# Groups of eight, four and two blocks in the gather of a relational graph layer, and other places for its short passes and weight pieces

## What is computed

```python
def _rgcn(x, edge_index, edge_type, weight, root, bias):
    src, dst = (edge_index[0], edge_index[1])
    msgs = x[src]
    out = x @ root + bias
    n = x.shape[0]
    for r in range(weight.shape[0]):
        mask = (edge_type == r).astype(x.dtype)
        sums = jax.ops.segment_sum(msgs * mask[:, None], dst, num_segments=n)
        cnt = jax.ops.segment_sum(mask, dst, num_segments=n)
        mean = sums / jnp.maximum(cnt, 1.0)[:, None]
        out = out + mean @ weight[r]
    return out
u = _rgcn(x, edge_index, edge_type, weight, root, bias)
z = jnp.concatenate([u, x], axis=1) @ w_gate + b_gate
h = jnp.tanh(u) * z + x * (1.0 - z)
```

## Time and profile before

| | us |
|---|---|
| median of 3 runs | 2188.13 |
| lowest and highest | 2180.44, 2189.11 |
| the profiled execution | 2187.53 |
| its span, first to last instruction | 2185.7 |
| mean granted TensorE clock | 0.956 of full |
| busy PE, DVE, ACT, POOL | 2011.1, 1284.4, 969.2, 904.0 |

### The profile page before, as it was taken

How to read it: one execution, slowest core, us unless ns; L and a number is a source line. 1 busy time by engine, 2 the same in 40 slices (tenths; PEclk the granted TensorE clock), 3 DMA queues, 4 the chain that set the end, 5 groups by cost and what they waited for, 6 DMA issues and landing times. The chain is left out here.

```text
span 2185.7 us, 28064 instructions
## 1 busy us (share of the span) xinstructions
PE 2011.1 (92%) x9425; PEld 1596.2 (73%) x9425; DVE 1284.4 (59%) x2282; ACT 969.2 (44%) x1506; POOL 904.0 (41%) x801
## 2 busy tenths in 40 slices
PE   8999999999999999999899899899799579899970
PEld 6777778778888888877677577677488468788860
DVE  8589588832222222139899899899798742222215
ACT  3211122222222222249899799899644223233332
POOL 0000046565655555237677588688200022212212
PEclk9999999999999999999899899999799779999995
DMA  5224487777777877679889799899565579998439
GB/s 185 100 81 134 137 272 247 259 251 253 254 258 259 256 258 256 227 223 321 273 292 315 242 329 319 272 331 313 194 178 176 199 266 326 305 318 287 103 75 188
DMA packets 156848, 520.96 MB, mean 238 GB/s; under 512 B 30748, under 2 KB 31132, under 8 KB 154672
## 3 DMA queue, kind: packets, MB, share of 16 engines
q1 hardware_dynamic: 85616, 310.51, 41.1%
q0 software_dynamic: 71104, 208.84, 32.1%
HBM read 383.83 MB, written 154.68 MB: 246 GB/s over the span
## 5 line engine op out<-in xcount | busy, mean ns | idle before, releaser
L211 PE MATMUL psum<-w_hi,xnT_hi 128*128 128x512 f32 (+1 forms) x1592 | 421.1, 399 | 4.6 <-PEq L228 2.5
L211 PE MATMUL psum<-w_lo,xnT_hi 128*128 128x512 f32 (+1 forms) x1592 | 417.8, 393 | 0.0
L211 PE MATMUL psum<-w_hi,xnT_lo 128*128 128x512 f32 (+1 forms) x1592 | 413.7, 394 | 0.0
L882 POOL DMA_INDIRECT sorted_rows<-acc x313 | 342.9, 1096 | 116.7 <-issue 85.3
L580 ACT ACTIVATE work<-psum 128x512 f32<-128x512 f32 (+1 forms) x150 | 89.7, 598 | 661.5 <-PE psum L211 661.5
L211 PEld LDWEIGHTS psum<-w_hi,xnT_hi 128*128 128x128 f32 (+1 forms) x1592 | 293.5, 187 | 75.4 <-issue 4.0
L211 PEld LDWEIGHTS psum<-w_lo,xnT_hi 128*128 128x128 f32 (+1 forms) x1592 | 294.9, 185 | 73.2
L211 PEld LDWEIGHTS psum<-w_hi,xnT_lo 128*128 128x128 f32 (+1 forms) x1592 | 294.3, 185 | 71.1
L982 POOL DMA_INDIRECT w_hi<-y_rows,sort_row x168 | 221.2, 1317 | 78.3 <-PE psum L1115 41.3
L982 POOL DMA_INDIRECT w_lo<-y_rows,sort_row x164 | 217.9, 1329 | 77.2 <-PE psum L1115 38.6
L1108 PE MATMUL psum<-y_hi,hot 128*128 128x512 f32 x664 | 220.0, 414 | 30.2 <-ACT y_hi L1030 27.4
(11 more groups left out here) (334 smaller groups left out, 2614.0 us busy)
## 6 DMA issues: line engine op xcount, KB each, us to landing
split_experts<-acc SPq DMA_DIRECT2D x128, 512.0 KB, 4.2
ring<-split_experts SPq DMA_DIRECT2D x16, 4096.0 KB, 16.1
w_raw<-in_wchunks SPq DMA_DIRECT2D x86, 512.0 KB, 5.0
y_rows<-work SPq DMA_DIRECT2D x144, 256.0 KB, 2.8
acc<-in_wchunks SPq DMA_DIRECT2D x64, 512.0 KB, 6.0
work<-local_rows SPq DMA_DIRECT2D x26, 384.0 KB, 4.2
sum_rows<-work SPq DMA_DIRECT2D x22, 256.0 KB, 4.5
acc<-in_bias SPq DMA_DIRECT2D x10, 512.0 KB, 5.5
```

What stands on the lines that cost most here:

```text
L211: i = pe.matmul(to[:rm, :], x_[:, k, m * P:m * P + rm], w_[:, s, k * HALF:(k + 1) * HALF], start=(n == 0), stop=(n == 3 * KD - 1))
L882: pool.indirect_dma_start(sorted_dram, IndirectOffsetOnAxis(ap=e_dest[:, c:c + 1], axis=0), e_rec[:, c, :], None, bounds_check=BLOCKS * P ...
```

## The change

The 332 blocks are grouped otherwise: 34 groups of eight blocks, 10 of four and 10 of two (at most one of four and one of two per tile), 54 groups in all. There are still 44 passes, of two "quads" each: a quad is four blocks (or two in a short pass), and a group of eight is the two quads of one pass, which sum in the same pair of banks (`BEGINS`, `ENDS`, `PAIR`) and are flushed once. Passes with two groups of four are 4, 10, 21, 32 and 39; short passes with two groups of two are 5, 11, 22, 33 and 43. In a short pass six matmuls of the unit stand between a block's high and low matmuls, so a unit still fits. The piece passes 8, 19, 30, 41 now have eight blocks: pieces 0 and 1 are split ahead of block 1, piece 2 ahead of block 6 and piece 3 ahead of block 7.

The sort has to find two kinds of rest per tile. `starts()` is cut into `starts()` at (1, 5), `shifts()` at (1, 8) and `owners()` at (3, 8), each with more small operations; `positions` has two more operations over 313 columns per tile, and takes one tile per step from (2, 1) to (3, 0).

```diff
-SHORT = GROUP // 2
-SHORT_GROUPS = TILES
-LONG_GROUPS = -(-((EDGES + TILES * (SHORT * P - 1)) // (SHORT * P) - SHORT_GROUPS) // 4) * 2
-GROUPS = LONG_GROUPS + SHORT_GROUPS
-BLOCKS = LONG_GROUPS * GROUP + SHORT_GROUPS * SHORT
+LONG, SHORT = 2 * GROUP, GROUP // 2
+SIDE_GROUPS = 2 * TILES
+LONG_GROUPS = -(-((EDGES + TILES * (SHORT * P - 1)) // (SHORT * P) - 3 * TILES) // 4)
+GROUPS = LONG_GROUPS + SIDE_GROUPS
+BLOCKS = LONG_GROUPS * LONG + TILES * GROUP + TILES * SHORT
+QUADS = 2 * LONG_GROUPS + SIDE_GROUPS
...
-                    link(v.tensor_scalar(t_odd_i, t_int, 1, None, ALU.bitwise_and))
+                    link(v.tensor_scalar(t_bit, t_int, 1, None, ALU.bitwise_and))
+                    link(v.tensor_copy(t_odd, t_bit))
+                    link(v.tensor_scalar(t_int, t_int, 1, None, ALU.logical_shift_right))
+                    link(v.tensor_scalar(t_bit, t_int, 1, None, ALU.bitwise_and))
+                    link(v.tensor_copy(t_mid, t_bit))
...
+                def shifts():
+                    v.tensor_tensor(mid_used, t_mid_start[:, TILES - 1:TILES], t_mid[:, TILES - 1:TILES], ALU.add)
+                    link(v.tensor_tensor(long_used, t_start[:, TILES - 1:TILES], t_groups[:, TILES - 1:TILES], ALU.add))
+                    v.scalar_tensor_tensor(out=t_mid_at, in0=t_groups, scalar=float(LONG * P), in1=t_off,
...
+                def owners():
+                    side = slice(LONG_GROUPS, GROUPS)
+                    v.tensor_scalar(side_odd, group_f[:, side], -1.0, float(GROUPS - 1), ALU.mult, ALU.add)
+                    v.tensor_scalar(side_mid[:, 0:TILES], group_f[:, LONG_GROUPS:LONG_GROUPS + TILES], float(-LONG_GROUPS), None, ALU.add)
...
                 def positions(first, last):
                     for t in range(first, last):
                         link(v.tensor_scalar(e_mask, e_tile, float(t), None, ALU.is_equal))
                         link(v.tensor_tensor_scan(e_scan, e_ones, e_mask, 0.0, ALU.mult, ALU.add))
-                        link(v.tensor_scalar(e_tail, e_scan, t_tail[:, t:t + 1], t_shift[:, t:t + 1], ALU.is_gt, ALU.mult))
+                        v.tensor_scalar(e_tail, e_scan, t_mid_at[:, t:t + 1], t_mid_shift[:, t:t + 1], ALU.is_gt, ALU.mult)
+                        link(v.tensor_scalar(e_last, e_scan, t_odd_at[:, t:t + 1], t_odd_shift[:, t:t + 1], ALU.is_gt, ALU.mult))
                         link(v.tensor_tensor(e_scan, e_scan, e_tail, ALU.add))
+                        link(v.tensor_tensor(e_scan, e_scan, e_last, ALU.add))
                         link(v.scalar_tensor_tensor(out=e_scan, in0=e_scan, scalar=t_off[:, t:t + 1], in1=e_mask,
                                                     op0=ALU.add, op1=ALU.mult))
...
-                side = {(HIST_CHUNK, 3): [turned], (HIST_CHUNK, 5): [starts],
-                        (HIST_CHUNK + 1, 2): [lambda: positions(0, 3)], (HIST_CHUNK + 1, 6): [lambda: positions(3, 6)],
-                        (HIST_CHUNK + 2, 0): [lambda: positions(6, 8)], (HIST_CHUNK + 2, 2): [lambda: positions(8, TILES)],
-                        (HIST_CHUNK + 2, 4): [records], (LOOK_CHUNK, 0): [table]}
+                side = {(HIST_CHUNK, 3): [turned], (HIST_CHUNK, 5): [starts], (HIST_CHUNK, 8): [shifts],
+                        (HIST_CHUNK + 2, 4): [records], (HIST_CHUNK + 2, 8): [owners], (LOOK_CHUNK, 0): [table]}
+                for t in range(TILES):
+                    side[(HIST_CHUNK + 1 + (t + 1) // TILES, (t + 1) % TILES)] = [lambda t=t: positions(t, t + 1)]
...
-        SHORT_PASSES = (*PIECES_AT, PASSES - 1)
-        ORDER, FIRST, COLUMN = [], [0], []
+        SHORT_PASSES = (*(i + 3 for i in PIECES_AT if i + 3 < PASSES), TILES // 2, PASSES - 1)
+        MID_PASSES = (*(i - 1 for i in SHORT_PASSES[:-1]), PASSES - 5)
+        assert not {*SHORT_PASSES, *MID_PASSES} & {*PIECES_AT}
+        KIND = [SHORT if i in SHORT_PASSES else GROUP if i in MID_PASSES else LONG for i in range(PASSES)]
+        BASE = {LONG: 0, GROUP: LONG_GROUPS * LONG, SHORT: LONG_GROUPS * LONG + TILES * GROUP}
+        NUMBER = {LONG: 0, GROUP: LONG_GROUPS, SHORT: LONG_GROUPS + TILES}
+        taken = {kind: 0 for kind in BASE}
+        OWNER, BEGINS, ENDS, PAIR, FIRST, COLUMN, pair = [], [], [], [], [0], [], -1
         for i in range(PASSES):
             for h in range(2):
-                short = i in SHORT_PASSES
-                n = sum((g >= LONG_GROUPS) == short for g in ORDER)
-                at, size = (LONG_GROUPS * GROUP + n * SHORT, SHORT) if short else (n * GROUP, GROUP)
-                ORDER.append(LONG_GROUPS + n if short else n)
-                COLUMN += range(at, at + size)
+                kind = KIND[i]
+                begins, ends = kind < LONG or h == 0, kind < LONG or h == 1
+                n, part = taken[kind], h * GROUP if kind == LONG else 0
+                pair += begins
+                OWNER.append(NUMBER[kind] + n)
+                BEGINS.append(begins)
+                ENDS.append(ends)
+                PAIR.append(pair)
+                at = BASE[kind] + n * kind + part
+                COLUMN += range(at, at + min(kind, GROUP))
                 FIRST.append(len(COLUMN))
+                taken[kind] += ends
         assert sorted(COLUMN) == list(range(BLOCKS))
 
         def size_of(g):
 
             return FIRST[g + 1] - FIRST[g]
 
-        def pieces_in(i):
-
-            return [(PIECES_AT[i], q) for q in range(PIECES)] if i in PIECES_AT else []
+        PIECES_BEFORE = {1: (0, 1), 6: (2,), 7: (3,)}
+
+        def pieces_in(i, n=None):
+
+            if i not in PIECES_AT:
+                return []
+            return [(PIECES_AT[i], q) for q in (range(PIECES) if n is None else PIECES_BEFORE.get(n, ()))]
...
-                        if pieces:
-                            c, q = pieces[n]
+                        for c, q in pieces_in(i, n):
                             act.wait_ge(mm_done, c * TILES)
                             hi_piece(act, c, 0, q)
...
-                        if g >= 1:
+                        if g >= 1 and ENDS[g - 1]:
                             flush(g - 1)
...
-                        if g >= 2:
-                            pe.wait_ge(acc_done, ACC_NO[g - 2])
+                        if BEGINS[g] and PAIR[g] >= 2:
+                            pe.wait_ge(acc_done, ACC_NO[PAIR[g] - 2])
+                        two = 2 * (PAIR[g] % 2)
...
-                            for _ in itertools.islice(steps, 3 * KD // SLOTS):
+                            for _ in itertools.islice(steps, 3 * KD // (FIRST[2 * i + 2] - FIRST[2 * i])):
```

More of the change, by code:

```diff
@@ L1065, in _ @@
                             b = j % SLOTS
-                            if pieces:
-                                lo_piece(v, pieces[j - FIRST[2 * i]][0], 0, pieces[j - FIRST[2 * i]][1])
+                            for c, q in pieces_in(i, j - FIRST[2 * i]):
+                                lo_piece(v, c, 0, q)
                             v.wait_ge(hi_done, j + 1)
@@ L1104, in _ @@
                             b, k = j % SLOTS, j - FIRST[g]
-                            first, last = k == 0, k == size_of(g) - 1
+                            first, last = BEGINS[g] and k == 0, ENDS[g] and k == size_of(g) - 1
                             pe.wait_ge(hi_done, j + 1)
                             for q in range(2):
-                                o = pe.matmul(bank[2 * h + q], hot[:, h, k, :], y_hi[:, j % 2, q * HALF:(q + 1) * HALF],
+                                o = pe.matmul(bank[two + q], hot[:, h, k, :], y_hi[:, j % 2, q * HALF:(q + 1) * HALF],
                                               start=first, stop=False)
                             o.then_inc(hi_used, 1)
-                            for _ in itertools.islice(steps, 3 * KD // SLOTS):
+                            for _ in itertools.islice(steps, 3 * KD // (FIRST[2 * i + 2] - FIRST[2 * i])):
                                 pass
@@ L1114, in _ @@
                             for q in range(2):
-                                o = pe.matmul(bank[2 * h + q], hot[:, h, k, :], slot_of(b)[:, q * HALF:(q + 1) * HALF],
+                                o = pe.matmul(bank[two + q], hot[:, h, k, :], slot_of(b)[:, q * HALF:(q + 1) * HALF],
                                               start=False, stop=last)
```

89 lines of the change are left out of this document (54 added, 35 removed).

## The result

| | before | after |
|---|---|---|
| median of the runs, us | 2189.1 (2180.4 to 2194.4, 9 runs) | 2175.4 (2172.6 to 2181.6, 9 runs) |
| ratio, 95% interval | 1 | 0.9948 [0.9933, 0.9964] |
| profiled execution, us | 2187.5 | 2177.2 |
| its span, us | 2185.7 | 2175.4 |
| first `y_hi` of the gather stage | 966.0 | 976.7 |

The change is worth 0.5% (11.4 us by the ratio); the time is 3.4 us above the forecast of 2172. But the two stages didn't both do what was forecast. The gather stage became 21.25 us shorter, and it begins 10.65 us later.

The account below looks back on a forecast made before the run. VectorE was taken to bound root passes and TensorE zx passes, with ACT close. Terms -3.3 - 15.6 - 6.2 + 1 + 1 + 6.7 = -16.4 gave 2171.1, 2172 as median; own range 2165 to 2179, wider range 2161 to 2184.

Parts of the forecast that it names:

- (a): Gather stage: 34 of 88 flushes go; 11 root passes gain 0.3 us each, 3.3 us in all, zx passes nothing.
- (b): Gather stage: product passes 5, 11, 22, 33 become short, 9.4 us each; 15.6 us gained.
- Rival 5: Root passes: the flush was not what set them, so the flush gain is 0; 2175 us, chance 0.07.
- Rival 4: Short passes aren't short, 10.9 us each from bank and one-hot turnaround; 6 us more, 2178, chance 0.08.
- The floor of 13.04 for a pass of 56 matmuls: Gather stage, TensorE: 8 x 1.63 us, below which a pass of 56 matmuls can't go.
- (c): Piece passes 8, 19, 30, 41 with eight blocks: the four places take 170.7 us against 176.9; 6.2 gained.
- (d): Half clock of TensorE at the piece passes: 0 to 2.5 us at each place, 1 us lost in all taken.
- (e): Transfers in piece passes: twelve of 512 KB at 374 GB/s may come late; 1 us lost in all, bounds 0 to 10.
- Rival 2: Piece passes bound in part by transfers at 325 GB/s; 9 us more, 2181, chance 0.12.
- rival 3: Piece passes: third piece's load queues behind gathers, landing over 6 us later than the 9.0 of before; 2201 us, chance 0.06.
- (f): Sort's side work on DVE: TensorE stands 5.2 us ahead of chunk 3, then 1.5 of half clock; 6.7 us lost.
- Rival 1: Front: TensorE doesn't stop ahead of chunk 3, so that loss falls to 0; 2165 us, chance 0.17.

Follow-up runs that it names:

- placement_only: Kernel before, with its groups of four and its front, but the new placement of short and piece passes; ratio to before 0.9943.
- grouping_only: Changed kernel with its groups of eight and its front, but the old placement of short and piece passes; ratio to before 1.0028.
- warm_pad: warm with group_tile made 34 unused words longer, so xnT stands where it does in the kernel before; 2160.5 us, ratio to before 0.9886.
- warm: spaced with 16 extra matmuls, results unused, in each piece pass (8, 19, 30, 41); 2163.4 us, ratio to before 0.9906.
- late_pieces: spaced with the third and fourth weight piece both ahead of block 7 of the piece passes; 2171.1 us, ratio to before 0.9942.
- spaced: Changed kernel with the sort's positions moved later, mostly one in every other step, records and owners at (3, 9); 2168.8 us, ratio to before 0.9911.

## Why the prediction held, point by point

The time was in the range and the sign right, but more than a third of the forecast gain didn't come: against the profiled execution, -16.4 was forecast and -10.3 measured. Terms that were 8.2 us too good were met by gains that were 2.1 better than forecast, and 3.2 of the 8.2 stand in no term of the sum. The gains and the stop were foreseen with their mechanism; that the time fell within the range owes something to its width of 14 us.

**Flushes (a) and short passes (b).** Right, and slightly under-sized. Passes 0 to 3 and 13 to 17 gained 3.9 us (0.4 each, not 0.3), the zx passes nothing. The four short places gained 17.1 us, of which (a) had put 0.6 on passes 6 and 12, so 16.2 was forecast. Together 21.0 against 18.9 (15.6 and 3.3). Rival 5, that the flush didn't set the root passes, is out: with 88 flushes (placement_only) they take 13.4, with 54 (grouping_only) 12.99. Rival 4, short passes of 10.9 us, is out too: it would have cost 6 us there. The floor of 13.04 for a pass of 56 matmuls was slightly high: such passes take 12.99, and 12.92 in warm_pad.

**Piece passes (c) and half clock (d).** Here the sum was wrong by 4.0 us: -6.2 with +1 and +1 was forecast, the changed kernel shows -0.2. The engines' work was sized rightly: (c) said 170.7 us for the four places, and at full clock they take 172.0 and 171.5. The step that failed is (d): "I take 1 in all" from a bound of 0 to 2.5 at each place, with the reason that twice the matmuls would shorten the half clock. They did shorten it: over the piece pass and the one behind, the granted clock is 0.84 to 0.89 in the changed kernel (0.83 to 0.95 in its second trace) and 0.66 to 0.81 in the kernel before. It still cost 4.9 us. The kernel before spent more time at the low clock, 0.50 for 17 us, while ACT and DVE waited for a load there; that these waits hid it, and that the full pass has none left to hide it in, is argued and wasn't tried. By the Trainium skill, "TensorE: Matmul & The Clock Gate", "Part 1", an array that idles falls to 1.2 GHz and runs its next matmuls at that; the windows at 0.66 and 0.50 agree.

**Transfers (e).** Between 1088 and 1095 us the queues moved 413 GB/s, and warm held 374 over 29.37 us of a piece pass and the one behind. So the 325 of the zx passes is no ceiling. Nor is the 358 that the prediction weighed, from the Trainium skill, "DMA: Bandwidth & Descriptors", "Where 436 GB/s comes from". The Trainium skill, "HBM Reference", "Specifications (TRN2)", has a core that streams alone well above its share, at about 425; these rows agree. Rival 2 is out, and so is rival 3: the third piece was taken 10.5 us behind the first (9.0 before), 1.5 later and not 6, and late_pieces shows that even its wait cost nothing.

**Front (f).** The mechanism and its place were right: a single stop, ended by the split of chunk 3's fourth piece, 5.0 us where 5.2 was counted; a position took 4.17 us (180.74 to 184.91 in order of time), 4.2 was counted. Half clock behind it cost 2.2 and not 1.5 (the unit takes 8.34 us, 208.93 to 217.27, where it took 6.11), since the second group of eight products was slow too; the three other traces with the stop show 1.4 to 2.7 for it. The second unit comes 7.4 us later than without the stop, against 6.7. Rival 1, that the front doesn't stop, is out.

**Not in the sum.** 3.2 us for the place of the buffers behind `group_tile` in SBUF. The prediction held matmuls for unchanged because their count and shapes were.

The sum of the misses: -2.1 (a, b), +4.0 (c to e), +0.7 (f), +3.2 (address), +0.3 behind the stage: 6.1, the difference of -16.4 and -10.3. It is the account of one pair of executions. Between the two traces of one kernel the first `y_hi`, the piece places and the part behind the stage differ by 0.2 to 2.4 us each, so a single term of it is known to 1 or 2 us.

**Chances.** The rival of chance 0.17, that the front doesn't stop, would have made 2165; spaced shows what that is worth, 2168.8.

## What to carry to other kernels

Where three engines are near their limit, count what a removed operation is worth as the distance to the next engine (0.4 of 1.13 us a flush), and read whether side work fits by adding it up from the last point where its engine can't save up work: a piece of work that was ready 5.2 us early before was done 10.6 us later, and TensorE stood 5.0 for it. A full pass laid where TensorE has little to do gets the engines' sum only while its clock stays up; idle time there is charged again behind it. And compare the start-to-start time of unchanged instructions in both traces first: a buffer that shrank ahead of an operand had put 3 us into the products, without a wait.

## What the runs showed of the hardware that I had not expected

- The start in SBUF of the buffers allocated behind `group_tile`, among them `xnT`, the 128-column operand that is loaded as weights, sets the pace of 512-column matmuls: 5.546 us for 24, or 5.567 with the buffers 120 to 136 bytes to one side or the other, 231.1 or 232.0 ns each. The 512-column operand didn't move.
- A core's queues moved 413 GB/s over 7 us (1088 to 1095 in the changed kernel) of gathers and loads of 512 KB together, and 374 over 29 us in warm.
- In warm and warm_pad 16 extra matmuls of 512 columns in a place (a piece pass and the one behind) with 89 made it 1.2 us shorter; the granted clock was 1.00 there, and 0.83 to 1.00 without them.
